# Low part of the rotated keys: one subtraction moved from VectorE to GpSimd (two-layer residual block with paged attention, one Trainium2 core)

## What is computed

```
x = x + x @ w_eff.T                 # weights quantized to a 64-entry codebook, plus a LoRA term
q, k, v = x @ Wq.T, x @ Wk.T, x @ Wv.T      # 32 query heads, 8 key and value heads, 128 wide
q, k = rope(rmsnorm(q)), rope(rmsnorm(k))
keys   = 512 cached keys (16 pages of 32) and the 32 new ones
probs  = softmax(q @ keys / sqrt(128)), masked to the cached length
x = x + (probs @ values) @ Wo.T
```

## Time and profile before

| | |
|---|---|
| median of 3 runs | 2198.47 us (2197.56 to 2199.87) |
| the profiled execution | 2198.64 us, of which the span of instructions is 2196.6 us |
| granted PE clock, mean | 0.993 of full speed |
| busy: PE, DVE, ACT, POOL | 96%, 79%, 67%, 57% of the span |

### The profile page before, as it was taken

The page is one execution under the profiler, slowest core; times in us unless marked ns, Lnnn a source line. Parts: engine busy times, 40 slices in busy tenths (PEclk is TensorE's granted clock), DMA queues, the critical chain, the costliest instruction groups (busy, mean ns, idle before and its releaser), DMA issues.

```text
span 2196.6 us, 60484 instructions
## 1 busy us (share of the span) xinstructions
PE 2113.5 (96%) x17634; PEld 1372.9 (63%) x17634; DVE 1735.5 (79%) x3933; ACT 1478.3 (67%) x4966; POOL 1244.7 (57%) x2070
## 2 busy tenths in 40 slices
PE   6979889999999999999999999999999999999998
PEld 2435466666666666666666666666666666666665
DVE  8976588887788888888876777778888778777785
ACT  4834577777777777767775666666677666666674
POOL 7011256666566666666665666566666566666563
PEclk9989999999999999999999999999999999999999
DMA  7987587887887887788888686666665666666663
GB/s 230 332 274 256 170 227 199 223 221 216 231 221 215 231 216 223 221 221 219 223 251 241 173 261 189 180 191 185 174 191 179 175 194 185 173 192 184 178 184 102
DMA packets 553805, 458.70 MB, mean 209 GB/s; under 512 B 127862, under 2 KB 482501, under 8 KB 552711
## 3 DMA queue, kind: packets, MB, share of 16 engines
q1 hardware_dynamic: 508038, 314.29, 51.8%
q0 software_dynamic: 40960, 134.25, 19.3%
q10 hardware_dynamic: 4480, 6.29, 0.9%
HBM read 377.21 MB, written 56.70 MB: 198 GB/s over the span
## 4 chain that ended last, share of the span: by engine, by line
PE 69%; DVE 8%; SPq 5%; issue 3%; ACT 1%; DMA 1%; DVEq 0%; ACTq 0%
PE PR L1334 16%; PE WOp L1367 14%; PE Op L1315 12%; PE Sp L1281 12%; PE PTp L1292 10%; SPq L755 3%; DVE split L1575 2%; PE TRp L1344 2%; DVE masked L1528 1%; PE Sp L1284 1%; DVE pts L1533 1%; PE Op L1297 1%; PE Op L1317 1%; DVE qr L1569 1%; DVE rs_ L1570 1%
## 5 line engine op out<-in xcount | busy, mean ns | idle before, releaser
L736 POOL DMA_INDIRECT pages<-values_split,rows x512 | 520.2, 1016 | 122.2 <-issue 109.2
L1334 PE MATMUL PR<-Wt,xT 128*128 128x512 f16 x2232 | 539.0, 380 | 0.0
L1418 ACT ACTIVATE pts<-PTp 128x512 f16<-128x512 f32 x512 | 305.7, 597 | 341.4 <-PE PTp L1292 340.6
L1315 PEld LDWEIGHTS Op<-pts,pages 128*128 128x128 f16 x6144 | 385.4, 98 | 129.4 <-DVE OT L1546 12.5
L1315 PE MATMUL Op<-pts,pages 128*128 128x128 f16 x6144 | 427.3, 219 | 9.3 <-DVE OT L1546 7.6
L1281 PE MATMUL Sp<-pages,qT 128*128 128x512 f16 x1536 | 416.4, 380 | 6.5 <-PEq L183 6.5
L1533 DVE TENSOR_TENSOR pts<-PTp,pts 128x512 f16<-128x512 f32 x512 | 351.2, 686 | 69.4 <-ACT pts L1418 69.2
L1528 DVE CUSTOM_DVE_ANT_0 masked<-Sp,mask 128x544 f32<-128x544 f32 x512 | 369.7, 722 | 44.2 <-PE Sp L1284 37.0
L1424 ACT ACTIVATE masked<-masked,small 128x544 f32<-128x544 f32 x512 | 379.7, 742 | 36.5 <-DVE small L1528 33.7
L1367 PE MATMUL WOp<-WoT,OT 128*128 128x512 f16 x1536 | 378.2, 379 | 0.0
L1292 PE MATMUL PTp<-ident,masked 128*128 128x128 f32 x2048 | 325.2, 281 | 14.5 <-DVE pts L1533 14.5
(11 more groups left out here) (252 smaller groups left out, 2967.8 us busy)
## 6 DMA issues: line engine op xcount, KB each, us to landing
pages<-keys_transposed SPq DMA_DIRECT2D x2048, 64.0 KB
mask<-mask_rows SPq DMA_DIRECT2D x128, 128.0 KB
v<-new_values SPq DMA_DIRECT2D x96, 128.0 KB
weights_split<-wsrc SPq DMA_DIRECT2D x40, 256.0 KB
keys_transposed<-pages SPq DMA_DIRECT2D x32, 256.0 KB, 5.2
values_split<-pages SPq DMA_DIRECT2D x16, 512.0 KB, 4.7
rope_s<-rope_table SPq DMA_DIRECT2D x32, 256.0 KB, 3.3
pages<-values_split,rows POOLq DMA_INDIRECT x512
```

The source lines that it names most:

```text
L736: nc.gpsimd.indirect_dma_start(out=vS[:, n % 2, c, :, :].rearrange("p l n -> p (l n)"), out_offset=None, in_=v_d, in_offset=bass.IndirectO ...
L1315: nc.tensor.matmul(o, vS[:, par, c, low, h * D:(h + 1) * D], pts[:, u % 2, part, c * P:(c + 1) * P], start=(k == 0), stop=False)
L1334: m = nc.tensor.matmul(bank(k), xT[:, c, xl, :], Wp[:, c, wl, GROUP_COL[k]:GROUP_COL[k] + HID], start=(i == 0), stop=(i == NPASS - 1))
L1418: nc.scalar.activation(pts[:, u % 2, 0, :], PTp[:, :], ACT.Copy).then_inc(G.pt_hi, 1)
```

## The change

The subtraction that makes the low part of the rotated keys leaves DVE's list and is put into POOL's list in slot 6, behind `add_rotated`. Operands, result and semaphores are the same. The SP queue with its transposing DMA is as before.

```diff
-    squares={1: 0, 3: 1, 6: 3, 8: 4, 10: 5}, values=5, values_low=6,
+    squares={1: 0, 3: 1, 6: 3, 8: 4, 10: 5}, values=5, values_low=6, keys_low=6,
...
                     def rotated_low(ti, tt, k):
-                        if k == 0:
-                            v.wait_ge(G.split_high, ti + 1)
-                            V.tensor_tensor(split[:, 1, :], qr[:, norm_no(ti, k) % 2, :], split[:, 0, :], ALU.subtract).then_inc(G.split_low, 1)
-                            return
                         v.wait_ge(G.tr_hi, turn_no(ti, k) + 1)
...
-                            if sl in plan["turned"]:
+                            if plan["turned"].get(sl, 0) != 0:
                                 rotated_low(ti, tt, plan["turned"][sl])
...
+                    def keys_low(ti):
+                        g.wait_ge(G.split_high, ti + 1)
+                        nc.gpsimd.tensor_tensor(split[:, 1, :], qr[:, norm_no(ti, 0) % 2, :], split[:, 0, :], ALU.subtract).then_inc(G.split_low, 1)
...
                         if ti in proj and sl in plan["add"]:
                             add_rotated(ti, plan["add"][sl])
+                        if ti in proj and sl == plan["keys_low"]:
+                            keys_low(ti)
```

## The result

The changed kernel takes 2179.80 us as the median of 6 runs (2174.78 to 2187.26), the kernel before 2199.52 in 6 (2197.56 to 2201.12). The ratio is 0.9913, with a 95% interval of 0.9895 to 0.9931. It is faster by 19.7 us. The profiled execution took 2179.6 us, its span is 2177.8.

What follows compares the result with a forecast made beforehand. PE, busy 96%, was taken to set the time. Waits of 13.8 us and 1.04 us removed sum to 14.8, so 2198.64 - 14.8 = 2183.8, predicted as 2183.7 us, range 2180.8 to 2188.

Steps and rivals of the forecast that it cites:

- PE's wait in slot 7: PE's probability transposes wait for DVE's probs_low, 0.46 us in each of 30 tile steps; claimed to go whole.
- The price of that wait: Gain from the transposes no longer waiting for probs_low, put at 30 x 0.46 = 13.8 us.
- 59.5 us: Forecast length of the tile steps after the change, given as a sign to look for.
- late tables: Rival: in the first 16 tile steps rope-table waits give back 16 x 0.46 = 7.4 us, 2191; 8 in 100.
- The bound of 2.7 us on POOL's time: A POOL subtraction above 2.7 us shuts out normalise(6), so o_low(3) comes late and PE waits in slot 7.
- The first tile step: PE's wait for the low part of a weight piece, made by DVE behind the subtraction, goes: 1.04 us.
- The range: The range for 8 in 10: 2180.8 to 2188 us, taking in part of the late tables.
- POOL's price: Each 128x512 subtraction on POOL taken as 1.27 us, hidden by idle time and costing nothing.
- The stretch of DVE's scaling: normalise(6) on DVE ends 0.30 us after POOL's subtraction, takes 1.28 us in place of 0.50, costing nothing.
- The slower rival: Slow mixed types on POOL shut out normalise(6); PE waits in slot 7, kernel slower beyond 3.15 us; 6 in 100.
- Its price at 3.81 us: With POOL's subtraction at three times the addition, a tile step loses 0.66 net, 31 of them give about 2219.

Runs made afterwards that it cites:

- Experiment 1: The kernel before, with the keys' subtraction still on DVE but behind probs_low, last in slot 6: 2182.73 us, ratio 0.9912.
- experiment 2: The kernel before with the keys' subtraction done twice on DVE, the second waiting for the first: 2220.47 us, ratio 1.0088.
- experiment 4: The changed kernel with POOL's keys' subtraction ahead of add_rotated in slot 6: 2211.70 us, ratio 1.0057 to the kernel before.
- experiment 6: The changed kernel with POOL's subtraction widened to three rows of 512 columns in one instruction: 2219.43 us, ratio 1.0010 to the kernel before.
- experiment 3: The changed kernel with POOL's subtraction cut to 4 of 512 columns from the second tile step on: 2179.01 us, ratio 0.9899 to the kernel before.
- experiment 7: The changed kernel run again unaltered: 2200.48 us, ratio 0.9924 to the kernel before.
- second and third set: Later runs, experiment 5 to the last; the kernel before took 2218.31 us in the second and 2217.02 in the third.
- experiment 5: The changed kernel with the keys' subtraction done twice or four times on POOL, with waits between: 2198.12 us, ratio 0.9915, and 2255.01 us, ratio 1.0164.
- first set: The runs of the first four experiments; the kernel before took 2200.38 us in them.

## Why the prediction was off

*That PE's wait in slot 7 is what the change is worth*: right. The entry is gone and no other has come. Experiment 1 shows that it was the place in DVE's queue, ahead of `probs_low` and beside POOL's addition, and that DVE's load played no part.

*The price of that wait*: this is the step that failed. "The whole wait goes: 30 x 0.46 = 13.8 us" took the idle time from the row. Start to start it was 0.61 us in a step, so the term is 30 x 0.61 = 18.3 us. The steps say the same: "59.5 us" was forecast for them, 59.94 - 0.46, and they take 59.34. The 30 tile steps that had the wait are 17.97 us shorter in all. In the second half each gives 0.60; in the first half they give between -0.55 and 1.37, since late tables and weight pieces fall differently in the two traces. Experiments 2, 4 and 6 show the same gap between written wait and price: 0.14, 0.22 and 0.18 us. The bound of 2.7 us on POOL's time has the same error, since it took 0.46 off the start of `values(4)`; with 0.61 it is 2.54, as experiment 6 gives.

*The first tile step*: the term of 1.04 us did not come. PE's wait for that weight piece is gone from the trace of changed, but a later piece, which comes by DMA, is there no sooner. PE starts to transpose it at 311.81 in both kernels, in the kernel before

```profile
311.81 0.66 PE L1352 MATMUL WOp<-ident,wsrc 128*128 128x128 f32 x4 [1.50 <-DMA wsrc<-in_L_cond_Wo]
```

and in the changed kernel

```profile
311.81 1.12 PE L1352 MATMUL WOp<-ident,wsrc 128*128 128x128 f32 x4 [1.95 <-DMA wsrc<-in_L_cond_Wo]
```

At the first piece the changed kernel gains 1.24 us, start to start. It had come there 0.79 us later than the kernel before, so it is 0.45 us ahead, and these 0.45 became a longer wait at 311.81, behind which the granted clock was at 0.57 from 311 to 315 us (1.00 in the kernel before). The transposes of group 1 serve as the mark of a step here. At those of the next tile step the changed kernel is 0.13 us behind. From there on it gains the 17.97 us, and 0.92 more behind the last tile step with a key group, mostly from one wait ahead of `values` (0.70 in place of 1.57 us): -0.13 + 17.97 + 0.92 = 18.76, the difference of the two spans.

*The sum put right*: with 0.61 in place of 0.46 it would have been 18.3 + 1.04 = 19.3, and the forecast 2179.2. That it lies 0.6 from the median is in part luck, since 1.04 of it was not there, 0.92 came from elsewhere, and the six runs spread over 12.5 us.

*The range*: it was built on the spread of the kernel before, 2.3 us. The changed kernel's runs spread over 12.5 us. In the profiled ones the rope table in tile step 14 was later than before, and PE stood 5.9 us in place of 3.9. Such waits differ from trace to trace: DVE's for the table came to 16.6 us in changed and to 23.8 in experiment 1.

*POOL's price*: taken as 1.27, measured 1.16 us. It changed nothing, as experiment 3 shows.

*The stretch of DVE's scaling*: forecast to 0.30 us after POOL's end, and there it is, 1.13 us long.

*The rivals*: late tables did not give the gain back (PE's waits for L1546 6.9 us against 5.2, the sum of the first 15 steps 9.1 us shorter). The slower rival's mechanism is real, its place right: with one POOL instruction of 3.1 us PE waits for L1546 in slot 7, and by estimate the wait begins near 2.5 us (experiment 6). POOL's real subtraction, 1.16 us, is too short for it. Its price at 3.81 us was worked out for a single instruction; several short ones cost by another way, through `root`.

What stays open is what makes the pauses of experiment 7, why the second and third set are 0.8% slower in all, and how much of a run's distance from another is the rope table alone.

## What to carry to other kernels

Price a wait of PE by the distance of two starts against the same two starts where nothing waits, not by the idle time written beside it: here 0.61 against 0.46, and times 30 that is 4.5 us, more than the whole miss of 3.9. A gain ahead of a transfer that comes no sooner is lost again in the wait for it, as in the first tile step. When an elementwise instruction of DVE takes over twice its usual time, look for a POOL instruction beside it, and move it behind that one before moving it to another engine: both did the same here. Whether work on POOL stays free for DVE is a matter of single instructions here, since one long one shuts DVE out for its whole length, while several short ones, each with a semaphore wait ahead of it, let it in.

## What was not expected of the hardware

POOL's f32 minus f16 to f16 of 128x512 took 1.16 us, less than its all-f32 addition, 1.27. Three times the width took 3.105, so 1.9 ns a column and about 0.19 us fixed; 4 columns took 0.204.

DVE's scaling, held up by POOL's subtraction, got in between two POOL instructions that had a semaphore wait and 0.07 us between them (1542.63 to 1542.70 in experiment 5). It was not tried without the semaphore wait.

In most traces of the second and third set ACT and DVE stand still for 0.9 us and more at some points of some tile steps, and no instruction of this core's profile has released them. In the changed kernel of experiment 7, waits from 1250 to 2090 us (the traces of the first set and of the two kernels of this study have no such rows):

```profile
ACT OT L1433 <- remote: 11.4, 7, 1.7
DVE masked L1528 <- remote: 10.0, 7, 1.5
ACT qn L1446 <- remote: 7.0, 7, 1.4
```

The undisturbed steps with such a pause are 0.3 us longer (experiment 7). No run tells what the pauses are.
